# Linear attention and soft routing: GpSimd scales the second token group, the normalisation steps at the stage boundary are moved, and a batch's first chunk updates the state first

## What is computed

```python
# attention without softmax: q, k, v are two-layer MLPs of x (gelu between)
scores = einsum('bid,bjd->bij', q, k) / scale
scores = scores * tril(ones)
out = einsum('bij,bjd->bid', scores, v)
out = (out - mean) * rsqrt(var + eps) * ln_w + ln_b
x = layernorm(x + out)                       # "z" in the kernel is x + out
# soft mixture of experts, 16 experts x 16 slots
xn = layernorm(x) * gamma + beta
logits = einsum('bnd,des->bnes', l2norm(xn) * scale, l2norm(mu))
dispatch = softmax over tokens;  combine = softmax over slots
slot_in = einsum('bnd,bnes->besd', xn, dispatch)
out = combine @ (gelu(slot_in @ w1 + b1) @ w2 + b2)
x = layernorm(x + out)
```

## Time and profile before

| | |
|---|---|
| median of 3 runs | 603.29 us (601.7 to 603.42) |
| the profiled execution | 603.0 us, its span 601.3 us |
| PE busy | 579.7 us, 96% |
| DVE busy | 478.5 us, 80% |
| ACT busy | 392.8 us, 65% |
| POOL busy | 344.2 us, 57% |

### The profile page before, as it was taken

The page is one execution under the profiler, slowest core; times in us unless marked ns, Lnnn a source line. Parts: engine busy times, 40 slices in busy tenths (PEclk is TensorE's granted clock), DMA queues, the critical chain, the costliest instruction groups (busy, mean ns, idle before and its releaser), DMA issues. The chain is left out here.

```text
span 601.3 us, 11764 instructions
## 1 busy us (share of the span) xinstructions
PE 579.7 (96%) x3844; PEld 531.7 (88%) x3844; DVE 478.5 (80%) x1012; ACT 392.8 (65%) x888; POOL 344.2 (57%) x359
## 2 busy tenths in 40 slices
PE   7989999999999999999999999977999999999995
PEld 5879999989999998999998999967899999988884
DVE  5698789788797897887978979878887777447786
ACT  3755766666767667667676766555877777535774
POOL 1738568577595585675956856466644444104443
PEclk9999999999999999999999999999899999999999
DMA  7324134042141340422413403204455555832444
GB/s 229 79 71 105 19 89 87 21 106 38 68 105 17 87 89 22 99 37 68 105 17 87 104 8 65 35 5 82 67 75 76 74 76 73 137 47 74 166 147 174
DMA packets 163473, 47.04 MB, mean 78 GB/s; under 512 B 139470, under 2 KB 159340, under 8 KB 163436
## 3 DMA queue, kind: packets, MB, share of 16 engines
q1 hardware_dynamic: 163424, 46.57, 35.4%
q10 hardware_dynamic: 12, 0.00, 0.0%
HBM read 21.39 MB, written 8.39 MB: 50 GB/s over the span
## 5 line engine op out<-in xcount | busy, mean ns | idle before, releaser
L511 POOL TENSOR_TENSOR h_lo<-xn_all,h_hi 128x512 fp32r<-128x512 f32 x32 | 41.4, 1292 | 114.2 <-ACT xn_all L595 114.1
L593 ACT ACTIVATE h_hi<-bank,bias_col 128x512 fp32r<-128x512 f32 x96 | 66.3, 691 | 32.9 <-PE bank L713 29.1
L711 PE MATMUL bank<-xnT_hi,w_hi 128*128 128x512 f32 x188 | 76.1, 405 | 0.0
L712 PE MATMUL bank<-xnT_lo,w_hi 128*128 128x512 f32 x188 | 74.4, 396 | 0.0
L713 PE MATMUL bank<-xnT_hi,w_lo 128*128 128x512 f32 x188 | 74.1, 394 | 0.0
L1510 PE MATMUL bank<-xn_all,e_tok 128*128 128x257 f32 x256 | 65.8, 383 | 0.0
L1084 DVE TENSOR_TENSOR state_lo<-bank,state_hi 128x512 fp32r<-128x512 f32 x57 | 39.2, 688 | 32.2 <-ACT state_hi L630 32.2
L630 ACT CAST state_hi<-bank 128x512 fp32r<-128x512 f32 x57 | 33.5, 588 | 37.1 <-PE bank L843 37.1
L1600 DVE STREAM_TRANSPOSE e_turn<-e_tok 128x256 f32<-128x256 f32 x64 | 40.5, 638 | 20.8 <-ACT e_tok L1414 20.2
L1588 PE MATMUL bank<-w_sb,ET_all 128*128 128x256 f32 x256 | 55.4, 379 | 0.0
L1414 ACT ACTIVATE e_tok<-bank,shift,xinv 128x256 f32<-128x256 f32 x64 | 36.2, 566 | 29.0 <-PE bank L1500 26.1
(11 more groups left out here) (188 smaller groups left out, 2054.3 us busy)
## 6 DMA issues: line engine op xcount, KB each, us to landing
x_all<-in_L_attn_x SPq DMA_DIRECT2D x16, 512.0 KB, 3.7
kT<-k_turn SPq DMA_DIRECT2D x128, 64.0 KB, 2.5
ET_all<-e_turn SPq DMA_DIRECT2D x64, 128.0 KB, 3.8
xn_all<-in_xT SPq DMA_DIRECT2D x15, 512.0 KB, 4.4
out<-xn_all SPq DMA_DIRECT2D x15, 512.0 KB, 3.0
w_sb<-in_L_ffn_w SPq DMA_DIRECT2D x2, 512.0 KB, 6.0
xn_all<-in_L_ffn_w SPq DMA_DIRECT2D x2, 512.0 KB, 6.8
xn_all<-in_xT SPq DMA_DIRECT2D x2, 256.0 KB, 3.8
```

Of the source, the lines that this page charges most:

```text
L511: pool.tensor_tensor(h_lo[:, V_SLOT, m, :], hv[:, m, :], h_hi[:, V_SLOT, m, :].bitcast(F32), ALU.subtract).then_inc(hv_split, 1)
L593: nc.scalar.activation(h_hi[:, h_slot(j, n), m, :], ps, ACT.Gelu, bias=bias(n, m))
L711: nc.tensor.matmul(ps, w[0], xs[0], start=start, stop=False, skip_group_check=shared)
L712: nc.tensor.matmul(ps, w[0], xs[1], start=False, stop=False, skip_group_check=shared)
```

## The change

1. Chunk order: in a batch's first chunk (i == 0) PE does `update_state` ahead of the `z_ready` wait and of `attend_chunk`. Other chunks keep their order.
2. GpSimd, group 15 of block 1: `add_beta(0, 0)` stands ahead of `split_hv(g, 1)`; `add_ln_b(15)` is done here, behind it, and no more in the last piece; then `divide_tokens(1, 1)` multiplies group 1's x1 by `r2_all`. In the last piece `weight_tokens(1)` multiplies by gamma, ahead of `add_beta(1, 1)`. `scale_tokens(1, 1)` on DVE is gone.
3. DVE `last_body`: sum, statistics and deviation of z of group 14 move from behind `mask_scores` to the end.
4. ACT, last piece: `apply_z(13)` moves from the end to two places between the roundings of the state, two tiles each.
5. DVE block 2: `split_xnT(1, 1)` goes between the pair statistics and the weight and add steps of group 15's first pair; `shift_z(14)` is done at t == 2, which puts it ahead of `scale_tokens(3, 3)`, instead of t == 3.

```diff
@@ gpsimd, block 1
-                def add_ln_b(g):
+                def add_ln_b(g, pairs=range(2)):
...
-                    for r in range(2):
+                    for r in pairs:
...
+                def divide_tokens(k, q):
+                    pool.wait_ge(x1_ready, GT * k + 3 * GT)
+                    pool.wait_ge(r2_ready, k + 3)
+                    pool.wait_ge(hv_split, 2 * GROUPS)
+                    pool.tensor_tensor(xn[q][:, :, 0:D], x1_all[:, GT * k:GT * k + GT, :],
+                                       r2_all[:, GT * k:GT * k + GT].unsqueeze(2).to_broadcast([P, GT, D]),
+                                       ALU.mult).then_inc(tok_divided, 1)
+
+                def weight_tokens(q):
+                    pool.wait_ge(tok_divided, 1)
+                    pool.tensor_tensor(xn[q][:, :, 0:D], xn[q][:, :, 0:D],
+                                       g_rows[:, :].unsqueeze(1).to_broadcast([P, GT, D]), ALU.mult
+                                       ).then_inc(tok_scaled, GT)
...
                         invert_norms(pool, 0, 0, minus_half[:, :])
-                        add_ln_b(a)
+                        weight_tokens(1)
                         add_beta(pool, 1, 1)
                         return
                     if project:
                         split_hv(g, 0)
                     if attend:
                         invert_o(pool, a, 0)
+                    if not more:
+                        add_beta(pool, 0, 0)
                     if project:
                         split_hv(g, 1)
...
-                        if attend and more:
+                        if attend:
                             add_ln_b(g)
                         if not more:
-                            add_beta(pool, 0, 0)
+                            divide_tokens(1, 1)
                         split_ktok(g, 0)
@@ scalar, block 1, last piece
                         preload(ba, i + 2)
+                        apply_z(act, a - 2, ja % 2, (0, 1))
                         round_state(ba, i + 2, tail_hi[2])
                         round_masked(a)
                         preload(ba, i + 3)
+                        apply_z(act, a - 2, ja % 2, (2, 3))
                         round_state(ba, i + 3, tail_hi[3])
                         nc.scalar.activation(warm[:, :], warm[:, :], ACT.Exp).then_inc(table_warm, 1)
-                        apply_z(act, a - 2, ja % 2, range(GT))
@@ tensor, block 1, chunk
                     if i == 0:
+                        update_state(a, c, True)
                         pe.wait_ge(z_ready, GT * a + 2)
                         last = attend_chunk(a, c, True, True)
...
+                    if 0 < i < TB - 1:
+                        update_state(a, c, False)
                     if i < TB - 1:
-                        update_state(a, c, i == 0)
                         carry(a, ba, i)
@@ vector, block 1, last_body
                     mask_scores(a)
-                    z_summed(dve, a - 1, 1)
-                    z_statistics(a - 1, 1 - p, 1)
-                    z_deviation(dve, a - 1, 1 - p)
                     tail_state(2)
                     split_masked(a)
                     split_xnT(dve, 0, 0)
                     tail_state(3)
-                    dve.wait_ge(hv_split, 2 * GROUPS)
-                    scale_tokens(1, 1)
+                    z_summed(dve, a - 1, 1)
+                    z_statistics(a - 1, 1 - p, 1)
+                    z_deviation(dve, a - 1, 1 - p)
@@ vector, block 2, route
-                        if first and t == 3:
+                        if first and t == 2:
                             shift_z(dve, a - 1, 1 - p)
@@ vector, block 2, ahead of route
                 def finish_out(a, r):
                     pair_statistics(dve, a, r)
+                    add_pair_out(a, r)
+
+                def add_pair_out(a, r):
                     weight_out(a, 2 * r)
...
                 scale_tokens(2, 2)
-                finish_out(GROUPS - 1, 0)
+                pair_statistics(dve, GROUPS - 1, 0)
                 split_xnT(dve, 1, 1)
+                add_pair_out(GROUPS - 1, 0)
                 floor_norms(dve, 1, 1)
```

More of the change, by code:

```diff
@@ L363, in build @@
             gam_rounded = asem("gam_rounded")
+            tok_divided = asem("tok_divided")
             gam_split = asem("gam_split")
```

## The result

The changed kernel takes 596.09 us in the median of 4 runs (595.15 to 597.5), the kernel before 602.57 us in four (601.7 to 603.42). The direction, the mechanism at the boundary and the place of the two stops came out. Three terms were mis-sized: the chunk order, the full clock behind the boundary, and the split that changed places.

A forecast was written before the change was run, and what follows sets the result against it. TensorE was taken as the bound, not full only around the block boundary. Chunk order 0.5, boundary 2.74 and block 2 1.55 made 4.8 us off the profiled 603.0: 598.2, plus 0.3 for the median, 598.5; range 596.3 to 601.0.

The forecast's parts named there:

- the mechanism at the boundary: Block boundary: TensorE ends last instead of GpSimd, its idle time falls from 2.53 to about 0.6 us.
- the place of the two stops: Block 2: TensorE stops about 1.1 us for an exponential, then 3.0 us for group 2's split.
- the chunk order: Each batch's first chunk: state products cover the 0.18 us wait for masked scores, 0.5 us gained over three batches.
- the full clock behind the boundary: Start of block 2: the low clock there should go, but gives little by itself since DVE has the longest work.
- the split that changed places: Block 2, DVE: group 1's split and half of finish_out swap at the same sum; 0.1 us charged for ScalarE's rounding.
- Reading of the bound: Whole kernel: TensorE is full away from the boundary; the change gains only what it takes from TensorE's gaps.
- The tail and the boundary: End of attention: the 0.77 us gap closes, GpSimd's late end goes, block 2's first matmul comes 2.74 us earlier.
- `shift_z`: Block 2, DVE: moved earlier it meets no open GpSimd pass, costs 0.15 instead of 1.80 us, 1.65 off the chain.
- The second low clock: Block 2, after the long stop at group 2's split: TensorE's clock most likely falls again, as before.
- Same cost: Block 2: the clock's fall after the long stop costs what it did before, so no term in the sum.
- Rival A: Block 2: the clock doesn't fall after the second stop, worth 1.2 us more, 597.3 us; chance 0.15.

The follow-up runs named there:

- the second profile: The unaltered changed kernel run again beside its parts on the same chip, against the kernel before: 596.21 us, ratio 0.9891.

## Why the prediction was wrong

Three steps failed: "three batches times 0.18 = 0.5", which measured 1.3; "that clock gives little by itself", put at nothing, which measured 1.28; and "I charge 0.1 us" for the split that changed places, which measured 0.9. They stand one by one below.

**Reading of the bound: right.** TensorE outside its stops is the bound; everything behind L16 is the same to 0.2 us in the profiles, and what was gained stands in the stretches around the stops.

**Chunk order: mechanism right, term mis-sized.** Forecast 0.5, measured 1.3: the step took the bracket for the cost. In the profiled execution of the changed kernel only 0.33 of it is seen. One part of the reason lies in its fourth batch, where `gam_lo` was held by two passes and the masked scores were late in spite of the new order:

```profile
317.46 2.52 DVE L1077 TENSOR_TENSOR gam_lo<-xn_all,gam_hi 128x4 fp32r<-128x4 f32 x1
```

```profile
317.43 2.53 POOL L524 TENSOR_TENSOR v_lo<-xn_all,v_hi 128x512 fp32r<-128x512 f32 x2
```

That group took 24.33 us instead of 23.6. Another group lost 0.28 us for a cause that stays open.

**The tail and the boundary: right, 3.0 for 2.74.** TensorE is last, all other ends lie ahead, and the barrier takes as long as before. The missing 0.27 is again what the bracket leaves out around the closed stop: about 1.05 us from start to start for its bracket of 0.77. GpSimd's product cost 1.90, below the 2.2 taken. The cover of 2.0 us behind it was confirmed by the two extra passes, and the offload's share by putting the scaling back. The moves of `apply_z(13)` and of z's steps were not tried one by one.

**`shift_z`: right.** 1.80 became 0.12, and alone it gave 1.8 us on DVE's chain. The hold by an open GpSimd pass explained it, and it explained four more places: `var_z` and `ve_z` with the shift alone, `nm_z` of group 15, `n_low`, and `gam_lo` above. The Trainium skill states the rule (SBUF — State Buffer, Who interferes with whom): a VectorE instruction with two SBUF inputs, or in a 2-port mode, and a GpSimd one that reads SBUF exclude each other. The traces agree: two-input and tensor-scalar instructions of 128x4 were held to the end of the pass (1.17 to 2.52 us), transposes and splits from PSUM beside the same passes kept their 0.64 us each. In which mode the tensor-scalar ones ran, no trace shows.

**"That clock gives little by itself, since DVE then has the longest work": wrong.** DVE's chain did start behind ScalarE's rounding of TensorE's transposes. With the full clock it started 1.28 us earlier (S + 5.33 instead of S + 6.61). I had looked at DVE from `turn_e` on, where it is full, and not at the two waits ahead of it.

**"At the same sum; I charge 0.1 us": wrong.** The swap costs 0.9. These two errors have opposite signs: forecast 1.55 for S to L8, measured 2.18, made of 1.8 for the shift, 1.28 for the clock and -0.9 for the swap. That 1.55 came so near is in part luck.

**The second low clock: half right.** It fell again after the long stop, as I said, in all three profiles of the changed kernel. "Same cost" was 0.5 us too low: before, the low stretch lay partly in a stop, now it lies wholly in work, and L8 to L16 takes 15.9 instead of 15.4; without a fall it is 14.3. Rival A, by which the clock stays up, is what the kernel without the swap showed in its profile.

Together, on the stretches of the second profile: 1.3 for 0.5, 3.0 for 2.74, 2.2 for 1.55, -0.5 for 0: 6.0 for 4.8. The medians differ by 6.5, with an interval of 5.1 to 8.1 us, so the last 0.5 us can't be told from scatter. The range was too narrow: its lower end made room for rival A, the clock in block 2, but gave the price of a stop and the clock behind the boundary none.

## What to carry to other kernels

Price a stop of TensorE by the starts of the matmuls around it, not by the idle time shown: here the stops of 0.18 and 0.77 us cost about 0.27 us more each, and stops of 2.4 us or more took the clock down in some executions, which cost 1.0 to 1.6 us. Small DVE instructions whose operands all lie in SBUF belong where no GpSimd pass is open; if one is held, look for what queues behind it, and check after a move that the hold hasn't gone to the next one. Before two steps change places, ask what each waits for, not only what both cost together.

## What was not expected of the hardware

The clock's fall is not decided by the length of the stop alone. At the boundary it fell after 2.53 us before and after 2.52 with the chunk order alone, but not after 2.53 with the shift alone nor after 2.59 with the scaling on DVE. In block 2 it fell after 2.42 us with the shift alone, but not after 2.42 without the swap, 2.59 with the scaling on DVE, or 2.89 with the chunk order alone. After the stops of 1.92 us or less in these profiles it did not fall. What decides it stays open. And GpSimd's product with a broadcast along the row took 1.90 us where the one with a broadcast across rows took 2.21; they also differ in the buffer they read, and which of the two matters was not tried.
